# Taking one in sixteen row maxima of an attention kernel over two PSUM banks at once

## The reference

```python
Q, K = _rope(Q, K)                      # Q, K, V = x @ W.T + b
scores = einsum('bhqd,bhkd->bhqk', Q, K) / sqrt(16)
w = softmax(scores, axis=-1)
x = layernorm(x + (w @ V) @ Wo.T + bo)
hdn = silu((x @ gate_w.T) * gate_s) * ((x @ up_w.T) * up_s)
x = layernorm(x + (hdn @ down_w.T) * down_s)
```

## Time and profile before

| | |
|---|---|
| median of 3 runs | 1011.74 us (1010.34 to 1012.72) |
| profiled execution | 1010.08 us, its span 1008.1 us |
| PE busy | 993.2 us (99%) |
| DVE busy | 803.6 us (80%) |
| ACT busy | 647.6 us (64%) |
| TensorE clock | 0.998 of full speed |
| attention with reductions | 24 to 711 us of the span |

### The profile page before, as it was taken

How to read it: one execution, slowest core, us unless ns; L and a number is a source line. 1 busy time by engine, 2 the same in 40 slices (tenths; PEclk the granted TensorE clock), 3 DMA queues, 4 the chain that set the end, 5 groups by cost and what they waited for, 6 DMA issues and landing times.

```text
span 1008.1 us, 17487 instructions
## 1 busy us (share of the span) xinstructions
PE 993.2 (99%) x6698; PEld 546.0 (54%) x6698; DVE 803.6 (80%) x1376; ACT 647.6 (64%) x1223; POOL 274.4 (27%) x284
## 2 busy tenths in 40 slices
PE   9999999999999999999999999999999999999996
PEld 4643435445434344443444444444368888888885
DVE  7999797998797999789899999999622666463635
ACT  5179796887787888788666688888852420322221
POOL 4361040241255540257210153565001001000002
PEclk9999999999999999999999999999999999999999
DMA  7174417234225531534140457331439113331011
GB/s 250 54 206 123 116 51 205 76 89 86 56 81 139 83 91 38 95 100 102 35 82 13 123 152 192 72 123 53 159 108 212 59 42 68 59 68 15 1 43 44
DMA packets 64297, 94.92 MB, mean 94 GB/s; under 512 B 37521, under 2 KB 37777, under 8 KB 62129
## 3 DMA queue, kind: packets, MB, share of 16 engines
q1 hardware_dynamic: 63920, 93.49, 36.5%
q10 hardware_dynamic: 288, 0.26, 0.1%
HBM read 53.88 MB, written 27.00 MB: 80 GB/s over the span
## 4 chain that ended last, share of the span: by engine, by line
PE 80%; DVE 15%; ACT 4%; issue 1%; DMA 1%; POOL 0%; DVEq 0%; POOLq 0%
PE PV L499 19%; PE PS L480 18%; PE PSA L570 16%; DVE nmx L1006 13%; PE PSA L458 6%; PE PS L587 6%; PE PS L402 4%; ACT Bn L802 3%; PE PS L526 2%; PE PSA L526 2%; PE PV L587 2%; PE PSA L402 1%; DVE nmx L1010 1%; PE PS L439 1%; DMA A<-in_wqk 1%
## 5 line engine op out<-in xcount | busy, mean ns | idle before, releaser
L1006 DVE TENSOR_REDUCE nmx<-PSA 128x1 f32<-128x512 f32 x976 | 592.6, 680 | 33.1 <-PE PSA L458 32.8
L802 ACT ACTIVATE Bn<-PS 128x512 f32<-128x512 f32 x898 | 476.5, 603 | 79.6 <-PE PS L480 72.5
L458 PE MATMUL PSA<-Kt,Qt 48*128 48x512 f32 x1010 | 359.7, 444 | 0.5 <-DVE nmx L1010 0.4
L480 PE MATMUL PS<-Qt,Kt 50*128 50x512 f32 x1006 | 341.8, 435 | 3.5 <-ACT Bn L802 3.0
L499 PE MATMUL PV<-Bn 128*32 128x256 f32 (+1 forms) x2696 | 298.0, 468 | 0.0
L480 PEld LDWEIGHTS PS<-Qt,Kt 50*128 50x128 f32 x1006 | 164.4, 184 | 240.8 <-ACT Bn L802 183.5
L458 PEld LDWEIGHTS PSA<-Kt,Qt 48*128 48x128 f32 x1010 | 165.7, 184 | 14.5 <-DVE nmx L1006 4.0
L570 PE MATMUL PSA<-x1Th,wr 128*128 128x512 f32 x344 | 135.3, 393 | 0.0
L570 PE MATMUL PSA<-x1Tl,wr 128*128 128x512 f32 x344 | 134.3, 390 | 0.0
L499 PE MATMUL PV<-P,Bn 128*32 128x512 f32 (+1 forms) x320 | 122.9, 466 | 0.0
L837 ACT ACTIVATE sg<-PSA,gs 128x512 f32<-128x512 f32 x43 | 29.6, 690 | 127.8 <-PE PSA L570 127.8
(11 more groups left out here) (177 smaller groups left out, 979.2 us busy)
## 6 DMA issues: line engine op xcount, KB each, us to landing
Qt<-pscr SPq DMA_DIRECT2D x90, 128.0 KB, 5.3
A<-in_wf SPq DMA_DIRECT2D x11, 768.0 KB, 5.5
wr<-A SPq DMA_DIRECT2D x33, 256.0 KB, 4.0
pscr<-A SPq DMA_DIRECT2D x16, 512.0 KB, 3.7
vscr<-Bn SPq DMA_DIRECT2D x32, 256.0 KB, 3.5
Kt<-pscr SPq DMA_DIRECT2D x90, 64.0 KB, 2.8
A<-A SPq DMA_DIRECT2D x16, 256.0 KB, 3.7
Bn<-vscr SPq DMA_DIRECT2D x8, 512.0 KB
```

The costliest lines, as they stand in the source:

```text
L458: op = e.matmul(slot_pair(s)[:, h, :], Qt[n % 3][p:p + NC_, g % 2, 128 * qt:128 * qt + 128], Kt[n % 3][p:p + NC_, 512 * h:512 * h + 512], ...
L480: e.matmul(score_tile(i), Kt[n % 3][rows, 128 * kt:128 * kt + 128], Qt[n % 3][rows, g % 2, 512 * qh:512 * qh + 512], start=True, stop=True ...
L802: e.activation(Pb[p_index(c)], score_tile(score_bank[c]), ACT.Exp, scale=0.25).then_inc(*act_exp.next(c))
L1006: e.tensor_reduce(col, slot_pair(s)[:, h, :], AX.X, ALU.max, negate=True).then_inc(*dve_max[s].next((k, 0) if h == 0 else k))
```

## The change

Of every sixteen steps, the one with k % 16 == 7 is taken whole again: 30 steps, 39 to 503. All others stay by halves. Since such a step writes only one of its two columns of `nmx`, the other columns (16 to 31) are set to 3.0e38 once at the start, so that the minimum in `join_max` takes the column that was written.

```diff
         def by_halves(k):
 
-            return k >= 24
+            return k >= 24 and k % 16 != 7
...
             e.memset(ones[:, :], 1.0).then_inc(*dve_const.next())
+            e.memset(nmx[:, :, 16:32], 3.0e38).then_inc(*dve_const.next())
             e.memset(half[:, :], -0.5).then_inc(*dve_const.next())
```

## The result

| | before | after |
|---|---|---|
| median of 6 runs each | 1011.78 us | 1015.35 us (1014.53 to 1016.81) |
| ratio to before | | 1.0038 (1.0027 to 1.0049) |
| profiled execution: time, span | 1010.08, 1008.1 us | 1016.81, 1014.8 us |

What follows compares the result with a forecast made beforehand. DVE was taken to pace plain sixteens, PE the background blocks. Blocks +2.7, casts +1.3 and plain steps -0.6 summed to +3.4 us on the 1011.74 us median: 1015.1 us, range 1010.0 to 1018.5.

Steps and rivals of the forecast that it cites:

- The bound: DVE sets the pace in sixteens without background work; at background blocks DVE idles 4.90 us and PE's time counts.
- 0.064 us saved for a step, by starts: On DVE, one whole reduction takes 1.13 us against 1.194 for two halves; thirty save 1.9 us if all arrives.
- Rival A: Saving arrives: PE's lateness is made up before each block, DVE's pace decides, 1009.8 us (1007.4 by recorded durations); chance 0.10.
- 0.43 us late, 0.18 taken off, 0.25 left: PE at step 457 h=0 is 0.43 us late; the vanished wait at 459 h=1 takes 0.18, leaving 0.25.
- Eleven blocks, +2.7, and five casts, +1.3: PE's 0.25 us lateness is passed on in full at 11 background blocks and 5 sixteens with ACT's casts.
- Fourteen plain steps, -0.6: The other 14 changed steps, without block or casts behind, gain 0.04 us each, -0.6 us in all.
- The sum: 2.7 + 1.3 - 0.6 = +3.4 us on the whole kernel, 1015.1 us against the median, +0.34%.
- DVE's idle time before L1006: DVE's idle time ahead of its reductions, 33.1 us before, to rise by some 5 us at blocks or first steps.
- Rival B: Nothing to be seen: delay made up at blocks or casts by half or more, -1 to +1.9 us; chance 0.22.
- C: Delay not made up at all: each of thirty steps costs 0.43 us, 12.9 in all, 1024.6 us; chance 0.08.

Runs made afterwards that it cites:

- experiment 4: Changed kernel with its thirty whole reductions at k % 16 == 2 instead of 7 (steps 34 to 498); ratio to before 0.9990.
- experiment 5: Changed kernel with its thirty whole reductions at k % 16 == 13 instead of 7, the first step behind a block; ratio to before 1.0047.
- Experiment 1: Kernel before, all steps by halves, but PE made to wait at 30 places for the step's second reduction; ratio to before 1.0055.
- experiment 2: Changed kernel with whole reductions only at the 16 places ahead of blocks or casts, plus a GpSimd memset; ratio to before 1.0040.
- experiment 3: Changed kernel with whole reductions only at the 14 plain places, plus a GpSimd memset; ratio to before 0.9990.
- experiment 7: Changed kernel with its thirty whole reductions at k % 16 == 3 instead of 7, farther from the block; ratio to before 1.0010.

## Why the prediction was right, point by point

- **The bound** (DVE in plain sixteens, PE in blocks): right. Where no bank came late, a saving on DVE did shorten plain sixteens, by 0.08 us in experiment 4 and by 0.04 to 0.08 in experiment 5, and was lost elsewhere; PE 0.25 us late at a block is 0.25 us more for that sixteen.
- **0.064 us saved for a step, by starts**: right, 1.13 us in the trace after. By the recorded durations it would have been 0.145, which none of the shortened sixteens shows. Rival A (faster) is out: the interval of the change lies wholly above 1. The some 125 ns that the Trainium skill ("Perfetto Trace Analysis", section "Optimizing Scalar/DVE Operations") gives for an instruction of DVE on PSUM do not fit this reduction, where merging two saves 0.064 us by the starts.
- **0.43 us late, 0.18 taken off, 0.25 left**: 0.43, and 0.25 left, in the trace after. Experiment 1 shows that the late bank alone makes a loss of this kind and more.
- **Eleven blocks, +2.7, and five casts, +1.3**: +3.1 and +1.35 by the joins of the change, +3.0 and +1.4 in experiment 2. So both terms are right, with 0.28 and 0.27 us for each place and not 0.25.
- **Fourteen plain steps, -0.6**: mis-sized. They gave 0.0 in the change and +0.1 in experiment 3. I had given DVE 0.03 us to spare at step 460 h=0; in fact it starts 0.08 us behind the end of the matmul's record, and the 0.06 saved go there.
- **The sum** of +3.4 was 3.6 by the medians and 4.4 in the trace by two decimals. The two errors go in one direction, 0.4 at the exposed places and 0.6 at the plain ones, and explain the 4.4. That the median came out within 0.3 us of the forecast is in part luck: it depends on how many runs fell into each group, and both groups say 4.2 to 4.5.
- **DVE's idle time before L1006** was to rise by some 5 us; it rose from 33.1 to 35.9. The remainder is in gaps that the recorded 0.68 us of a reduction covers in part or whole: between the first and the last join, what the distances of starts without a recorded gap have over 0.597 us (1.13 for a whole reduction) sums up to 2.5 us before and 4.5 after. 2.8 + 2.0 = 4.8 us.
- **Rival B** (made up by half or more) and **C** (never made up) are out by the joins: plain ones did not grow, those with a block or a cast grew by the full 0.25.

The joins are those of one profiled execution for each kernel. How far they scatter: in the change and in experiments 2 and 3 the plain sixteens but the last agree with before within 0.02 us.

## What to carry to other kernels

One wide read of two buffers in place of two narrow ones saves the reader, here 0.064 us by the starts, and keeps the first buffer 0.54 us longer. Look at who fills that buffer next: the room between its release and its next use, and behind it the nearest place where lateness can't be made up. With room (experiment 4), or farther ahead with more waiting places between (experiment 7), it was free; three u ahead of a block, what the one waiting place between leaves of the lateness (0.25 of 0.43 us) is paid in full. And take the cost of an instruction on a saturated engine from the distance of starts, not from recorded durations.

## What the runs showed that I had not expected

- PE's total time of waiting does not give the loss: 10.3 us of new waits (7.0 net of old ones that vanished) cost 0.0 us in experiment 7, 10.7 us cost 4.3 in the change.
- Between two profiled executions the first join shifted by up to 2.3 us (65.6 and 67.9 us) with no difference in the program ahead of it but one memset. The memset isn't the cause: experiment 4 has it, with a first join at 65.2 us, and experiment 1 has it not, with 67.5. DVE's first work with the cosines began at 9.96 us before and here, in the changed kernel, at:

```profile
11.91 1.53 DVE L967 SCALAR_TENSOR_TENSOR A<-PSA,bqk,A 64x512 f32<-64x512 f32 x2 [3.93 <-PE PSA L402]
```

  What made it late is not shown. A difference of spans of that size means nothing before it is split at a common point.
